# Mixer tensors in DRAM by token, then sequence: one transfer for a chunk of all sequences

## What is computed

```python
r = sigmoid(x_r @ W_r.T + b_r).reshape(B, T, H, D)
k = l2norm((x_k @ W_k.T + b_k).reshape(B, T, H, D))
v = l2norm((x_v @ W_v.T + b_v).reshape(B, T, H, D))
def step(state, (r_t, k_t, v_t)):            # over the 256 tokens
    pred = einsum("bhij,bhj->bhi", state, k_t)
    err = pred - v_t
    state = dec * state - et * (err[..., :, None] * k_t[..., None, :])
    n = sqrt(sum(state * state over i, j))
    state = state * where(n > max_norm, max_norm / n, 1)
    return state, einsum("bhij,bhj->bhi", state, r_t)   # wkv
wkv_n = groupnorm(wkv) * gn_weight + gn_bias            # per sequence and head
out = (wkv_n @ W_o.T + b_o) * g
```

## Times and profile before

| | us |
|---|---|
| median of 3 runs | 6758.13 |
| the 3 runs | 6751.82 to 6759.17 |
| profiled execution | 6756.8 |
| its span, first to last instruction | 6755.0 |
| busy in the span: PE, DVE, ACT, POOL | 5962.8, 5530.5, 3576.0, 3730.7 |
| mean granted TensorE clock | 0.949 |

### The profile page before, as it was taken

The page is one execution under the profiler, slowest core; times in us unless marked ns, Lnnn a source line. Parts: engine busy times, 40 slices in busy tenths (PEclk is TensorE's granted clock), DMA queues, the critical chain, the costliest instruction groups (busy, mean ns, idle before and its releaser), DMA issues. The chain is left out here.

```text
span 6755.0 us, 179966 instructions
## 1 busy us (share of the span) xinstructions
PE 5962.8 (88%) x76324; PEld 4338.5 (64%) x76324; DVE 5530.5 (82%) x10471; ACT 3576.0 (53%) x8048; POOL 3730.7 (55%) x1761
## 2 busy tenths in 40 slices
PE   7566666799998899999999999999788789999999
PEld 5466665677777755555555555555566578888888
DVE  7798998555547879999999999999666588777886
ACT  5455554333333478888888888878355522222221
POOL 1576776111111169999999999999422122222232
PEclk9777777899999999999999999999899999999999
DMA  3232221111102331121112111111121100000000
GB/s 102 73 77 65 54 52 53 37 48 44 41 14 104 124 89 38 52 51 44 46 37 58 42 50 42 44 46 30 54 85 57 35 20 8 8 8 8 8 8 7
DMA packets 390641, 314.64 MB, mean 47 GB/s; under 512 B 171686, under 2 KB 358569, under 8 KB 389324
## 3 DMA queue, kind: packets, MB, share of 16 engines
q1 hardware_dynamic: 384150, 302.84, 15.4%
q10 hardware_dynamic: 5686, 0.29, 0.1%
HBM read 194.99 MB, written 108.01 MB: 45 GB/s over the span
## 5 line engine op out<-in xcount | busy, mean ns | idle before, releaser
L2386 POOL TENSOR_TENSOR ss_ch<-ss_h,ss_c_all 128x2048 f32<-128x2048 f32 x511 | 2325.6, 4622 | 33.9 <-DVE ss_h L2415 23.2
L2415 DVE TENSOR_TENSOR_SCAN ss_h<-ss_decay,banks 128x1024 f32<-128x1024 f32 x1024 | 2256.6, 2267 | 64.1 <-PE banks L2302 63.5
L2302 PE MATMUL banks<-ss_diag,ss_dxT 128*32 128x256 f32 x32768 | 1970.3, 381 | 25.8 <-DVE ss_h L2415 17.1
L2302 PEld LDWEIGHTS banks<-ss_diag,ss_dxT 128*32 128x32 f32 x32768 | 1008.0, 110 | 808.3 <-DVE ss_h L2415 196.1
L2366 ACT ACTIVATE ss_decay<-ss_dt,ss_neg_a 128x510 f32<-128x510 f32 x2048 | 1358.1, 710 | 257.5 <-DVE ss_h L2415 251.3
L2754 POOL TENSOR_TENSOR pk_blockhot<-pk_onehot,pk_parts 128x2048 bf16<-128x2048 bf16 x96 | 345.5, 3628 | 935.7 <-DVE pk_parts L2980 935.7
L2357 ACT ACTIVATE ss_diag<-ident,ss_bT 128x128 f32<-128x128 f32 x2016 | 685.2, 387 | 184.4 <-PE banks L2302 184.4
L812 PE MATMUL banks<-ms_rprod,ident 128*128 128x128 f32 x2048 | 465.4, 399 | 315.0 <-POOL ms_rprod L936 309.3
L2309 PE MATMUL banks<-ss_ch,ss_stacked 128*32 128x256 f32 x8192 | 635.5, 382 | 45.2 <-POOL ss_ch L2386 40.3
L812 PEld LDWEIGHTS banks<-ms_rprod,ident 128*128 128x128 f32 x2048 | 431.6, 258 | 342.5 <-POOL ms_rprod L936 278.3
L1045 POOL TENSOR_SCALAR l_ln_mv<-l_ln_mv 128x2 f32<-128x2 f32 x64 | 15.1, 236 | 985.0 <-DVE l_ln_mv L1040 985.0
(11 more groups left out here) (330 smaller groups left out, 9998.2 us busy)
## 6 DMA issues: line engine op xcount, KB each, us to landing
ss_dt<-keep_dt SPq DMA_DIRECT2D x256, 128.0 KB, 4.0
ss_c_all<-keep_cn SPq DMA_DIRECT2D x512, 64.0 KB, 2.1
keep_v<-ms_cx_values SPq DMA_DIRECT2D x32, 512.0 KB, 2.8
l_va<-keep_v SPq DMA_DIRECT2D x32, 512.0 KB, 4.4
l_kf<-keep_k SPq DMA_DIRECT2D x32, 256.0 KB, 2.8
keep_x<-l_x SPq DMA_DIRECT2D x32, 256.0 KB, 2.1
keep_xc<-si_xc SPq DMA_DIRECT2D x16, 512.0 KB, 3.5
keep_zs<-si_zs SPq DMA_DIRECT2D x16, 512.0 KB, 4.5
```

The lines of the kernel that those rows point to most:

```text
L2302: m = T_.matmul(inp[u % 2][s * CB:(s + 1) * CB, g, :, t * P:(t + 1) * P], inputs[i % 2][0][:, g, t, u * CB:(u + 1) * CB], diag[slot][:, g, ...
L2386: G_.tensor_tensor(ch[u // 2 % 4][:, :, :, :, :].rearrange("p j g n t -> p j (g n t)"), h[u // 2 % 4][:, :, :, :, :].rearrange("p j g n t ...
L2415: V.tensor_tensor_scan(whole(h[u // 2 % 4][:, u % 2, :, :, :]), whole(decay[u % 4]), whole(inp[u % 2]), 0.0, ALU.mult, ALU.add).then_inc(s ...
```

## The change

r, k, v and wkv lie in DRAM as (token, sequence, channel); g keeps its layout. A token of all sequences is then 16 KB in one piece, in the order of the partitions, so load_steps and store each issue one transfer of 128 partitions where they issued sixteen, and the semaphores count one. The stores of stage 1 and the loads of wkv in stage 3 take the rows of one sequence, which are 1 KB long as before and now 16 KB apart instead of 1 KB.

```diff
-            S.dma_start(rows(dr[c][b]), z.res[:, n, :, :]).then_inc(z.stored.sem, DMA)
+            S.dma_start(rows(dr[c][b] if c == "g" else dr[c][:, b, :]), z.res[:, n, :, :]).then_inc(z.stored.sem, DMA)
...
-    steps = [st.mark(f"steps_loaded{n}", 3 * B * DMA) for n in range(2)]
+    steps = [st.mark(f"steps_loaded{n}", 3 * DMA) for n in range(2)]
...
+    def by_heads(name, c):
+        return dr[name][tokens(c)].rearrange("t b c -> t (b c)").rearrange("t (p x) -> p t x", p=P)
...
-        for b in range(B):
-            of_chunk = dst[:, c % RING, :, :, :] if name == "r" else dst[:, tokens(c), :, :]
-            engine.dma_start(of_chunk[b * HP:(b + 1) * HP, :, :, :].rearrange("h t e d -> h t (e d)"),
-                             dr[name][b][tokens(c)].rearrange("t (h x) -> h t x", h=HP)).then_inc(steps[c % 2].sem, DMA)
+        of_chunk = dst[:, c % RING, :, :, :] if name == "r" else dst[:, tokens(c), :, :]
+        engine.dma_start(of_chunk.rearrange("p t e d -> p t (e d)"), by_heads(name, c)).then_inc(steps[c % 2].sem, DMA)
...
-        for b in range(B):
-            ps = slice(b * HP, (b + 1) * HP)
-            S.dma_start(dr["wkv"][b][tokens(c)].rearrange("t (h x) -> h t x", h=HP),
-                        WKV[ps, c % 2, :, :, :].rearrange("h t e d -> h t (e d)")).then_inc(stored[c % 2].sem, DMA)
+        S.dma_start(by_heads("wkv", c), WKV[:, c % 2, :, :, :].rearrange("p t e d -> p t (e d)")).then_inc(stored[c % 2].sem, DMA)
...
-            S.dma_start(wkv[b % 2][:, :, :], rows(dr["wkv"][b])).then_inc(wkv_loaded[b % 2].sem, DMA)
+            S.dma_start(wkv[b % 2][:, :, :], rows(dr["wkv"][:, b, :])).then_inc(wkv_loaded[b % 2].sem, DMA)
...
-    dr = {n: dram(n, (B, T, C)) for n in ("r", "k", "v", "g", "wkv", "x1", "x2", "x3")}
+    dr = {n: dram(n, (B, T, C)) for n in ("g", "x1", "x2", "x3")}
+    dr |= {n: dram(n, (T, B, C)) for n in ("r", "k", "v", "wkv")}
```

More of the change, by code:

```diff
@@ L748, in mixer_scan @@
     measured, spread_root, spread_ready = st.mark("measured"), st.mark("spread_root"), st.mark("spread_ready")
-    norm_spread, norm_ready, stored = st.mark("norm_spread"), st.mark("norm_ready"), [st.mark(f"wkv_stored{n}", B * DMA) for n in range(2)]
+    norm_spread, norm_ready, stored = st.mark("norm_spread"), st.mark("norm_ready"), [st.mark(f"wkv_stored{n}", DMA) for n in range(2)]
     def tokens(c):
         return slice(c * CH, (c + 1) * CH)
+    def by_heads(name, c):
+        return dr[name][tokens(c)].rearrange("t b c -> t (b c)").rearrange("t (p x) -> p t x", p=P)
     def load_steps(engine, c, name, dst):
```

## The result

Over 7 runs each, measured side by side, the changed kernel takes 6734.69 us (6731.97 to 6736.14) and the kernel before 6756.35 us: a ratio of 0.9967, with a 95% interval of 0.9956 to 0.9979. A second comparison, on another occasion, gave 6732.55 against 6753.94 (0.9968, 0.9956 to 0.9980). The kernel is faster by some 21.5 us, as forecast in sign, but by more than the 17.0 of the forecast and 1.3 us outside of the range's lower end. The profiled execution is the median run; its span is 6732.9 us against 6755.0.

The account below looks back on a forecast made before the run. It took the scan's recurrence to bound the kernel, with transfers exposed only at its start, Folding's boundaries, its end and stage 3's first load. 7.2 + 8.1 + 2.2 - 0.5 = 17.0 us less gave 6741, range 6736 to 6751.

Parts of the forecast that it names:

- What bounds the kernel: Stage 2: the recurrence, some 900 us, doesn't move; transfers are waited for only at start, Folding's boundaries and end.
- One transfer: A single transfer of 2048 pieces of 128 bytes replaces sixteen issues of 6.1 us, using 16 engines instead of 8.
- t: Time for the data of one merged 262 KB transfer: taken as 1.4 us, with ends 0.7 and 6.0.
- Rivals 1 and 4: Rate goes by queue or piece, t near 6.0: 6758, chance 0.10; large transfers block the queue, t = 8: 6773, 0.04.
- The start: Start of stage 2: DVE's first sum at 217.7 instead of 224.95, loads deciding; gain 7.2 us, at most 8.0.
- the formula: Start of stage 2: the last of k, v and r lands at about 208.8 + 0.5 + 3t + 1.4 = 214.9.
- Folding: Four chunk boundaries, 9.7 us of excess: PE's wait goes, its products still take 3.68 us; gain 8.1 us.
- rival 2: Folding's boundaries: the loads come as late again and the wait stays, leaving 8.9 us of gain, 6749; chance 0.12.
- The end: End of the scan: the last store lands before the group norm's chain is done; gain 2.2 us.
- Rows 16 KB apart: Stage 1's last stores and stage 3's first wkv load: loss taken as 0.5 us, between 0 and 5.
- rival 3: Rows 16 KB apart move at half the rate: 12.5 us less in all, 6746; chance 0.06.
- The sign named for being wrong: Stage 1 ending later than 208.8 by over 1 us would show the prediction wrong.

Follow-up runs that it names:

- e3_store: Changed kernel with the loads of k, v and r left as sixteen transfers, stores of wkv merged; 6741.88 us, ratio 0.9984.
- e4_fold_first: Kernel before, with SP issuing Folding's store and two loads ahead of the sixteen stores of the mixer's chunk; 6742.79 us, ratio 0.9986.
- e8_half: Kernel before, with Folding's store and two loads issued between the eighth and ninth of the sixteen stores; 6740.13 us, ratio 0.9978.
- e1_layout: Changed kernel's layout with the sixteen transfers of before, one for each sequence, for loads and stores; 6755.19 us, ratio 1.0001.
- e2_loads: Changed kernel with the stores of wkv left as sixteen transfers, loads merged; 6749.27 us, ratio 0.9994.
- e5_tokens: Changed kernel with sixteen transfers for each chunk, each one token of all 128 partitions; 6761.29 us, ratio 1.0013.
- e7_start: Changed kernel with r's load issued ahead of the two rate loads and the context's fills moved from DVE to POOL; 6731.03 us, ratio 0.9969.

## Why the prediction was wrong

Sign and places held, and so did the mechanism but for one step: how long PE's products take once nothing is waited for. That term of the sum was sized too low. Against the account above:

1. **What bounds the kernel: right.** All of the scan outside of the three places moved by 0.5 us.
2. **One transfer: right.** t was 1.4 and is 1.2 us, with 16 completion marks. Rivals 1 and 4 are out. One reading was off without harm: the stores of the earlier trace rows move 512 KB and not 256, but k's load of 256 KB takes 0.36 us to issue as well.
3. **The start: right in size, in part by luck**, 7.1 us against 7.2. The loads decide and DVE follows 0.5 us behind (worked out: 0.8). The last load is in use 6.3 us after the first issue where the formula gave 6.1, but with the measured t the formula gives 0.5 + 3.6 + 1.4 = 5.5: it had no term for the two small loads, behind which r goes out 1.4 us late, and that and the high t came out even.
4. **Folding: the failed step.** It said: "its products still take 3.68 us and ACT waits for them, so the excess falls by PE's wait and no further", 8.1 us. Measured 9.9 in the change, and an excess of zero in e3_store, e4_fold_first and e8_half. The products' 3.68 us were not theirs but a result of the wait I was taking away: at the granted clock of 0.50 behind an idle PE; without the wait they take 1.91 at 1.00. I had the row of the first boundary with 2.00 us, named it as the case of a higher gain, and didn't ask why two rows of the same work differ. The loads' time to landing was no problem (rival 2 is out). The lead was smaller than worked out: the keys' load goes out 3.55 us behind the context's last store (506.79 - 503.24) where it was 7.80 (516.42 - 508.62), 4.3 us sooner and not 6.1, because Folding's store took 2.10 us to issue. Three microseconds are enough (e8_half), so this cost nothing.
5. **The end: right**, 2.4 us against 2.2.
6. **Rows 16 KB apart: nothing that shows** where I took 0.5; e1_layout has it in time and profile, and rival 3 is out. The sign named for being wrong, stage 1 ending over 1 us late, did come, but the delay was there before the first such row.
7. **The sum.** The right terms give 7.1 + 9.9 + 2.4 = 19.4, and stage 2 measured 19.9, against 17.0 forecast for the whole. Of the 6.3 us between the forecast time and the measured one, Folding is 1.8 and the rows 0.5. Another 1.8 are no part of the kernel: I started from 6758.13, the median of three runs, and the seven runs beside the changed kernel gave 6756.35. As a gain my range was 7 to 22 us, and the measured 21.7 lies at its end. The rest is in stages that the change doesn't touch, a balance that nothing here explains. Between the kernels here, the difference between the timed gain and stage 2's gain runs from -3.4 us (e2_loads) to +4.0 (e8_half). My range ended 1.3 us above the measured time: it was made from the terms' ends and left 2 us for the starting point and such a balance together. Without either one of the two the measured time would lie within it.

## What to carry to other kernels

When a wait for a transfer goes away, ask what the engine behind it did at a lower clock because of the wait; take its duration from a row where it came without a gap. Two rows of the same work with different durations, as 2.00 and 3.68 us here, are the sign to look for. On a queue that issues many small transfers the cost sits in what stands behind them, and moving one urgent load ahead (one line, e4_fold_first) gave half of what the new layout gave. A view of who waits for a transfer, over the whole stage and not only over its ends, finds such places.

## What the runs showed of the hardware that I had not expected

- A transfer of 16 KB over 128 partitions costs SP 0.48 us to issue and one over 8 partitions 0.38, although both have 128 pieces (e5_tokens); it isn't the layout, since e1_layout has it too and takes 6.09 us for sixteen of 8 partitions.
- A large transfer of small pieces is itself issued in 0.47 us; it is the next one in the queue that takes longer to issue: 2.10 us for Folding's store behind the one of 2048 pieces, against 0.35 us in e8_half. It took 1.9 us off the lead of Folding's loads and did no harm here.
- The small loads of the rates, issued behind r's 256 KB, were the last to land (e7_start); issued ahead of it, r's was. One of the two is late in either order.
